# Last attention of a two-layer transformer kernel: keys and queries brought in by halves, and a new order of the work around it

## The reference

```python
x = x + attn0(_ln(x))          # 8 heads, softmax over queries
x = x + ffn_fp4(_ln(x))        # 704 wide, blockwise FP4 rounding
x = x + attn1(_ln(x))          # 16 heads of 16; q and k normalised per head
x = x + moe(_ln(x))            # base matmul + top-2 of 8 rank-16 adapters

def attn1(x):
    qkv = x @ w_qkv + b_qkv
    q = ln(q, g_q, be_q) * HD ** (-0.5);  k = ln(k, g_k, be_k)
    out = softmax(q @ k.T) @ v
    return out @ w_proj + b_proj
def moe(x):
    gate = top2(softmax(x @ R.T));  gate = gate / (gate.sum() + 1e-6)
    return x @ W.T + b + einsum(gate * (x @ A.T), B)
```

## Time and profile before

| | us |
|---|---|
| runs before, median of 3 (lowest to highest) | 3127.02 (3123.2 to 3137.87) |
| the profiled execution | 3126.74 |
| its span in the trace | 3124.9 |
| granted TensorE clock over the span | 0.96 of full speed |
| PE busy / DVE / ACT / POOL | 2703.7 / 2142.0 / 1961.6 / 1299.8 |

### The profile page before, as it was taken

How to read it: one execution, slowest core, us unless ns; L and a number is a source line. 1 busy time by engine, 2 the same in 40 slices (tenths; PEclk the granted TensorE clock), 3 DMA queues, 4 the chain that set the end, 5 groups by cost and what they waited for, 6 DMA issues and landing times.

```text
span 3124.9 us, 62704 instructions
## 1 busy us (share of the span) xinstructions
PE 2703.7 (87%) x23854; PEld 1237.8 (40%) x23854; DVE 2142.0 (69%) x4363; ACT 1961.6 (63%) x3701; POOL 1299.8 (42%) x1645
## 2 busy tenths in 40 slices
PE   4875887998899988999889988999889998998696
PEld 2433443335433444334433344334443344333232
DVE  6878766848787577856688477866779476765333
ACT  3541355875577755876568755776558755786683
POOL 4752375216732366215542166324652156412111
PEclk9987998999999999999999999999999999999797
DMA  4213241424222332224313242333323252132311
GB/s 124 60 20 61 45 97 37 80 43 104 47 68 59 70 89 71 55 41 93 82 50 76 47 108 50 75 48 74 94 57 67 34 105 56 46 67 38 83 28 27
DMA packets 474142, 201.33 MB, mean 64 GB/s; under 512 B 287561, under 2 KB 463441, under 8 KB 473817
## 3 DMA queue, kind: packets, MB, share of 16 engines
q1 hardware_dynamic: 471544, 195.12, 28.9%
q10 hardware_dynamic: 2272, 1.85, 0.2%
HBM read 46.61 MB, written 32.51 MB: 25 GB/s over the span
## 4 chain that ended last, share of the span: by engine, by line
PE 49%; DVE 26%; issue 7%; ACT 7%; POOL 4%; DMA 4%; SPq 3%; DVEq 0%; ACTq 0%; POOLq 0%
PE pV L634 10%; PE pR L425 7%; PE pS L489 7%; DVE nmaxa L1115 7%; PE pR L426 6%; PE pR L427 6%; PE pS L605 6%; ACT ub L859 4%; PE pV L522 4%; PE pR L431 2%; SPq L1774 2%; DVE ua L1027 1%; POOL ua L1570 1%; DMA xT<-xhb 1%; ACT ua L820 1%
## 5 line engine op out<-in xcount | busy, mean ns | idle before, releaser
L859 ACT ACTIVATE ub<-pS 128x512 f32<-128x512 f32 x2048 | 1047.9, 612 | 258.2 <-PE pS L605 255.2
L1115 DVE TENSOR_REDUCE nmaxa<-pS 128x1 f32<-128x1024 f32 x512 | 621.2, 1214 | 342.9 <-PE pS L489 342.1
L820 ACT ACTIVATE ua<-pS,nmaxa 128x1024 f32<-128x1024 f32 x384 | 427.6, 1113 | 519.9 <-DVE nmaxa L1115 507.7
L1570 POOL TENSOR_SCALAR ua<-ua,rz 128x256 f32<-128x256 f32 x512 | 493.3, 964 | 502.5 <-DVE rz L1132 465.1
L489 PE MATMUL pS<-ua 128*128 128x512 f16 x2048 | 545.0, 390 | 93.5 <-ACT ua L820 77.3
L634 PE MATMUL pV<-ub,vaug 128*17 128x512 f32 x4096 | 542.9, 601 | 8.5 <-DVE ub L1266 8.5
L605 PE MATMUL pS<-ub 50*128 50x512 f16 x1920 | 351.6, 385 | 41.0 <-SPq L1977 24.1
L522 PE MATMUL pV<-ua 128*32 128x128 f32 x6144 | 253.6, 285 | 53.4 <-DVE oTa L1126 33.5
L489 PEld LDWEIGHTS pS<-ua 128*128 128x128 f16 x2048 | 164.9, 99 | 337.4 <-ACT ua L820 111.4
L820 ACT ACTIVATE EA<-pS,nmaxa 128x1024 f32<-128x1024 f32 x128 | 142.5, 1114 | 169.8 <-DVE nmaxa L1115 169.8
L605 PEld LDWEIGHTS pS<-ub 50*128 50x128 f16 x1920 | 86.7, 94 | 410.0 <-ACT ub L859 315.1
(11 more groups left out here) (289 smaller groups left out, 5169.6 us busy)
## 6 DMA issues: line engine op xcount, KB each, us to landing
ua<-ua SPq DMA_DIRECT2D x384, 128.0 KB, 2.6
ub<-scr SPq DMA_DIRECT2D x276, 64.0 KB, 2.5
scr<-ub SPq DMA_DIRECT2D x30, 512.0 KB, 3.2
x<-in_L_attn_x SPq DMA_DIRECT2D x8, 1024.0 KB, 5.6
between<-x SPq DMA_DIRECT2D x7, 1024.0 KB, 5.1
ub<-between SPq DMA_DIRECT2D x7, 1024.0 KB, 5.9
out<-ub SPq DMA_DIRECT2D x7, 1024.0 KB, 5.3
ub<-scr SPq DMA_DIRECT2D x168, 32.0 KB, 1.9
```

What stands on the lines that cost most here:

```text
L820: e.activation(EA[n % 4], pS[:, 1024 * (n % 2):1024 * (n % 2) + 1024], ACT.Exp, bias=nmaxa[:, n % 32:n % 32 + 1], accum_out=zz[:, n % 8:n ...
L859: e.activation(EB[(4 * n + hl) % 8], pS[:, 512 * hl:512 * hl + 512], ACT.Exp).then_inc(e1_in, 1)
L1115: e.tensor_reduce(nmaxa[:, n % 32:n % 32 + 1], pS[:, 1024 * (n % 2):1024 * (n % 2) + 1024], AXX, ALU.max, negate=True).then_inc(max0_in, 1)
L1570: e.tensor_scalar(vs[m % 4], vv[:, :, 32 * c:32 * c + 32], rz[:, c:c + 1], None, ALU.mult).then_inc(vs_in, 1)
```

## The change

1. `heads_end` of SP brings the first 512 keys, then head group 0's first 512 queries (new `half_queries`), then the second half's tiles; `attn1` starts on the first and waits for `keys_late` at step 4 and for `fill1_late` at steps 32 and 40.
2. On DVE, `by_norm` of pairs 0 and 1 comes ahead of the Newton iteration of pairs 2 and 3 (`heads_by_end`), and the low parts are a lane of their own.
3. POOL's bias adds wait until the last low part is made.
4. PE's wait for `mrow` is on the `If` side only.
5. `second` places the mixture by a table (`at_step`) in place of the formulas.

```diff
--- before.py
+++ after.py
@@ -204,7 +204,9 @@
 
         s1_in, e1_in, pv1_in, o1_in, rc_in = (sem(n) for n in ("s1", "e1", "pv1", "o1", "rc"))
         fill1 = [sem(f"fill1_{i}") for i in range(2)]
-        fill1_end = [sem(f"fill1_end{i}") for i in range(2)]
+
+        fill1_end, fill1_late = ([sem(f"fill1_{n}{i}") for i in range(2)] for n in ("end", "late"))
+        keys_late = sem("keys_late")
         keys_in, ones_in = sem("keys"), sem("ones")
         gsm, gmax, gT, ghi, glo, mrow = (sem(n) for n in ("gsm", "gmax", "gT", "ghi", "glo", "mrow"))
 
@@ -343,10 +345,16 @@
 
 
             if b == NB - 2:
-                return [placed(lambda p: 66.5 + min(p, .43 * p + 5.4), lane(b))]
+                return [placed(lambda p: at_step(p, (66.5, 75.5, 79.5, 83.5, 89.5, 96, 103)), lane(b))]
             if b == NB - 1:
-                return [placed(lambda p: -26.8 + min(p, .42 * p + 2.9), lane(b, 0)), placed(.5, lane(b, 1))]
+                return [placed(lambda p: at_step(p, (-26, -21, -18, -13.5, -11, -7.5, 2)), lane(b, 0)), placed(.5, lane(b, 1))]
             return [lane(b)]
+
+        def at_step(p, to):
+
+            of = (0, 10, 17.7, 19.5, 30, 39, 62)
+            n = max(i for i in range(6) if p >= of[i])
+            return to[n] + (p - of[n]) * (to[n + 1] - to[n]) / (of[n + 1] - of[n])
 
         def tiles_in(hf):
             return range(NT) if hf is None else range(4 * hf, 4 * hf + 4)
@@ -559,12 +567,15 @@
                 e.wait_ge(*group_in(b, hg))
                 q, kk_ = operands(b, hg)
                 if hg == 0:
-                    e.wait_ge(keys_in, 384 * (b + 1) - (192 if b + 1 == NB else 0))
+                    e.wait_ge(keys_in, 384 * b + (384 if b + 1 < NB else 96))
                     e.wait_ge(ones_in, 2)
                 if k == 0:
                     e.wait_ge(fin, 1)
                     e.reg_load(reg, flag[0:1, 0:1])
                 with e.If_cmp(reg, 0, "IS_NE"):
+                    if b + 1 == NB and hg < 2:
+                        e.wait_ge(keys_late, 96)
+                        e.wait_ge(fill1_late[hg], 96)
                     if hg or b + 1 == NB:
                         e.wait_ge(e1_in, 256 * b + 4 * group_step(b, hg))
                     else:
@@ -580,6 +591,7 @@
                             i.then_inc(gsm, 1)
                     e.wait_ge(gmax, 32 * k + 32)
                     transpose(pS[0:32, 0:128], nmaxb[:, :]).then_inc(gT, 1)
+                    e.wait_ge(mrow, 64 * (k + 1))
                 with e.Else():
                     e.sem_inc(gsm, 32)
                     e.sem_inc(gT, 1)
@@ -592,8 +604,11 @@
                         if n == group_step(b, hg):
                             yield n - .1
                             general(b, hg)
-                            e.wait_ge(mrow, 64 * (4 * b + hg + 1))
                         yield n
+                        if b + 1 == NB and n == 4:
+                            e.wait_ge(keys_late, 96)
+                        if b + 1 == NB and n in (32, 40):
+                            e.wait_ge(fill1_late[hg], 96)
                         for hl in range(4):
 
                             if n or b + 1 == NB:
@@ -1418,12 +1433,17 @@
                     e.wait_ge(sq_in, 4 * b + tp + 1)
                     e.tensor_reduce(nve[tp // 2][:, 64 * (tp % 2):64 * (tp % 2) + 64],
                                     sqe[tp].rearrange("p (g d) -> p g d", d=16), AXX, ALU.add).then_inc(hs_in, 1)
-                    if tp == 3:
-                        e.wait_ge(hs_in, 4 * b + 4)
-                        newton(e, nr_in[1], nve[1], nye[1], nwe[1])
+                yield sums_end(3) + .3
+                e.wait_ge(hs_in, 4 * b + 4)
+                newton(e, nr_in[1], nve[1], nye[1], nwe[1])
+
+            def heads_by_end():
                 for tp in range(4):
-                    yield (sums_end(2) + .5, sums_end(3) + .2)[tp // 2]
+                    yield sums_end(3) + .1 + .4 * (tp // 2)
                     by_norm(e, tp, 0).then_inc(hmd_in, 1)
+
+            def heads_low_end():
+                b = NB - 1
                 for tp in range(4):
                     yield turn_end(tp) + .2
                     for w_ in range(2):
@@ -1530,7 +1550,7 @@
                         *([placed(-10, prep()), placed(-10, prep_low()), prep_heads()] if i < 0 else []),
                         *([v for lane in (moe_x3, moe_gate, moe_M) for v in second(i - 1, lane)] if within(i - 1) else []),
                         *([heads(i), heads_bias(i), heads_norm(i)] if within(i) and i + 1 < NB else
-                          [heads_end(), heads_bias(i), heads_norm_end()] if i + 1 == NB else [])]
+                          [heads_end(), heads_bias(i), heads_norm_end(), heads_by_end(), heads_low_end()] if i + 1 == NB else [])]
 
             phases(lanes_x, lanes_y)
 
@@ -1687,6 +1707,9 @@
                 for t in range(NT):
                     yield 20 + .1 * t
                     xb = x[b % 2][:, t, :]
+                    if t == 0:
+
+                        e.wait_ge(lo1_in, 8 * NB)
                     e.wait_ge(xh_in["H"], 8 * b + t + 1)
                     e.tensor_tensor(xb, xb, bproj[:, :], ALU.add).then_inc(xb1_in, 1)
 
@@ -1902,15 +1925,26 @@
                     yield turn_end(2 * hf + 1) + .4
                     for i in range(2):
                         e.wait_ge(spill[i], 32 * b + 16 * (hf + 1))
+                    cols = slice(512 * hf, 512 * hf + 512)
                     for par in range(2):
                         for s_ in range(3):
                             at = 64 * par + 16 * s_
-                            e.dma_start(kop[at:at + 16, :, 512 * hf:512 * hf + 512],
-                                        scr[b % 2, 1, s_ % 2, 0:128, 512 * hf:512 * hf + 512].rearrange(
-                                            "(h p d) n -> p d h n", p=2, d=16)[par]).then_inc(keys_in, 16)
-                yield 19
+                            e.dma_start(kop[at:at + 16, :, cols], scr[b % 2, 1, s_ % 2, 0:128, cols].rearrange(
+                                "(h p d) n -> p d h n", p=2, d=16)[par]).then_inc((keys_in, keys_late)[hf], 16)
+                    if hf == 0:
+                        half_queries(b, 0, 0)
+                half_queries(b, 1, 0)
                 for hg in range(2):
-                    queries(b, hg, False)
+                    half_queries(b, hg, 1)
+
+            def half_queries(b, hg, hf):
+                o, cols = 2 * (hg % 2), slice(512 * hf, 512 * hf + 512)
+                for par in range(2):
+                    for s_ in range(3):
+                        at = 64 * par + 16 * s_
+                        e.dma_start(qop[at:at + 16, o:o + 2, cols],
+                                    scr[b % 2, 0, s_ // 2, 64 * hg:64 * hg + 64, cols].rearrange(
+                                        "(h p d) n -> p d h n", p=2, d=16)[par]).then_inc((fill1, fill1_late)[hf][hg], 16)
 
             def heads(b):
                 if b:
```

## The result

| us | before | after |
|---|---|---|
| median (lowest to highest), 6 runs each, taken together | 3126.32 (3123.08 to 3137.87) | 3103.22 (3096.75 to 3112.54) |
| the profiled execution | 3126.74 | 3096.75 |
| its span | 3124.9 | 3095.0 |
| in it: from the start to the last of DVE's sums of squares (the body) | 2880.2 | 2868.2 |
| from there to the first score matmul (the gap) | 35.9 | 25.2 |

The changed kernel takes 0.9924 of the time, 95% interval 0.9900 to 0.9949: 23.1 us less, more than the 0.5% that can be told from nothing. The two profiled executions differ by 30.0 us: 12.0 in the body, 10.7 in the gap, 6.8 in the attention, 0.5 in the tail.

A forecast was written before the change was run, and what follows sets the result against it. Bound by a serial chain in the gap, then PE and ACT together in the last attention. Terms 11.5 + 5.5 + 2.2 + 0.3 + 1.9 - 0.8 - 0.9 = 19.7 us, from 3126.74 to 3107, range 3099 to 3119.

The forecast's parts named there:

- the wait for SP: Outside the last attention, PE's five idle times of 3.8 us go; half taken as gain, 1.9 us.
- my own case: Whole kernel: the main forecast, 13.4 to 24 us gained by its own bounds, 3103 to 3113; chance 0.63.
- The start: Last attention's first score matmul comes at 2904.5 where it was 2916.05, 11.5 us earlier; bounds 9.4 to 13.
- Step 4 doesn't wait: Last attention: late keys land at 2913.1, step 4's scores come at 2915.3, which leaves 2.2 us.
- the rival with the start handed back: Last attention, step 4 or later: six reads delay the late puts' landing; gain only 12 us, 3115; chance 0.17.
- The table: Last attention's mixture: gains of 5.5 (router tile), 2.2 (ghT) and 0.3 us, less 0.8 and 0.9.
- the new wait at image 7's projection: Last attention: image 7's transposes wait for image 6's base tile 7, now at step 37.0; costs 0.8 us.
- The 2.2 for ghT: Image 6's ghT: 5.4 steps from the last router tile remove the 1.76 us wait, plus 0.45 for a slow step.
- The rival "saves nothing": Last attention: PE is full and moved work lands there; only start and SP wait gain, 3115; chance 0.12.
- SP doesn't become the bound: Against the rival that slow SP reads delay image 6's transposes: 3138, decided from 0.94 us a read; chance 0.03.
- My 3.5 for this rule: In the gap, DVE's first two by_norm would take 3.5 us by the rule, not 2.8; gain 10.8.
- my terms of 0.45: Last attention: slow step behind a removed wait goes too; 0.45 us counted behind image 6's ghT, likewise at the router tile.

The follow-up runs named there:

- after_mrow_back: The changed kernel with PE's wait for mrow put back where it was: 3127.89 us, ratio 1.0000.
- act_queries: The changed kernel with the first six reads of queries issued from ACT's queue beside SP's keys: 3106.3 us, ratio 0.9935.
- late_and_table2: The changed kernel with twelve query reads behind image 6's transposes, ghT's exponential earlier for both images, image 7's projection later: 3099.0 us, ratio 0.9913.
- late_reads: The changed kernel with only the twelve reads of the queries' second half moved behind image 6's DMA transposes on SP: 3094.09 us, one execution.
- after_again: The changed kernel, unchanged, executed once more for a second trace: 3102.93 us.
- after_no_halves: The changed kernel with keys and queries read in full as before, without late waits: 3113.31 us, ratio 0.9961.
- mrow_only: The kernel before with only PE's wait for mrow moved to the If side: 3119.81 us, ratio 0.9973.
- table_only: The kernel before with only the table that places the mixture: 3123.05 us, ratio 0.9989.
- before_again: The kernel before, unchanged, executed once more for a second trace: 3130.04 us.

## Why the prediction was right, and where it was not

I forecast 3107, in a range of 3099 to 3119, and 3103.22 was measured: 19.7 us against 23.1. The mechanism of each large term was seen in the traces. That the total came so near owes something to luck: start and attention were forecast 1.8 us too high together, the wait for SP 2.3 too low. (The upper bounds of my own case add up to 24.8 and not to 24, which would have made its lower end 3102.) Step by step:

1. **The start, 11.5 forecast, 10.7 measured** (trace; 35.9 to 25.2). Counted from the last sum of squares, `by_norm`, the iteration and the low parts brought the second put 2.4 us nearer (forecast 2.05): DVE's two multiplications took 2.15 and not 2.8, and the low parts 3.35 and not 3.5. But SP's first read came 3.96 us after the second put's issue began (2881.92 to 2885.88) where I carried over the 3.28 of before. That is the step that failed: I took a landing as a constant although the two puts now start 1.2 us apart and not 2.3 (2894.04 to 2896.30 before). And the first scores came 2.46 us after the last issue where I had 2.1. The removals divide the 10.7: halves 8.3, POOL's wait 0.9, DVE's order 0.6; with the 0.6 that the wait for SP is worth alone (gap 35.3) that is 10.4. This division holds only with the wait gone: put back, it costs 14.8 us of gap (40.0).
2. **Step 4 doesn't wait**, as forecast. The late keys' puts let SP go on 6.3 us after the second's issue (2891.9 to 2898.16), not 4.66, and the rival with the start handed back came nearer than I thought: last issue near 2900.4, landed some 2 us later, needed at 2903.95. 1.5 us were left of my 2.2. The rival gave the six reads ahead of the puts as the reason. They are not: `after_mrow_back` has the same reads there, and SP goes on after 4.7 us. What the seven traces with 6.3 us have in common, and the seven others (4.7, in `act_queries` 5.3) have not at that place, is one packet of 16 KB of instructions that goes over the DMA engines while the put is under way, 2.5 to 2.7 us after PE has started the attention. The DMA engines' busy tenths, in 40 slices, and that packet in the changed kernel, from 2894 to 2899 us:

```profile
DMA  9999898999999999200000000000000000000000
...
q8 instruction: 1, 0.02, 1.2%
```

and the busy tenths in `after_mrow_back` over the same stretch of its puts, 2902.4 to 2907.4 us, which has no such packet:

```profile
DMA  9999998989999999610000000000176118613663
```

In both nearly all of the put is over some 2.1 us into the stretch. Without the packet SP goes on 0.5 us later (2904.99), with it 2.0 later (2898.16), though the engines are all but idle meanwhile. No run takes the packet away, so that it is the cause is likely and not shown.
3. **The table.** My 6.3 for the attention stands against 5.3 (162.7, the mean of two traces of before, to 157.4). The router's wait went from 4.63 to 0.58, and the new wait at image 7's projection is 0.94, forecast 0.8. **The 2.2 for ghT failed**: it waits 1.48. I counted the steps between router and ghT in PE's order, but the chain to ghT starts with the gate's exponential, and when that runs is set by its place in ACT's order. `late_and_table2` moves that place, among other edits, and the wait is gone. Without the table PE lost 7.04 us at the router tile, so the table was worth more in the changed kernel (8.0 us in the trace) than I gave it, and less alone (0.9989). The rival "saves nothing" fell.
4. **The wait for SP, 1.9 forecast.** This term was undersized. Over fourteen traces the last sum of squares starts 4.2 us earlier where the wait is gone (a fit with the time at the low clock beside it, uncertain by 0.9; last section). So about all of the 3.8 us came back, not half. Why none of it is lost to ACT, no run shows. More important is what I counted at nothing: that without this part the halves would gain nothing. I had drawn the count-up behind the reads the earlier trace rows, but never asked what each part is worth without the others.
5. **SP doesn't become the bound.** The 18 late reads took 9.24 us, 0.51 each, far from the 0.94 at which it would have decided.

The sum by what was measured: 10.7 + 5.3 + 4.2 = 20.2, of 23.1 measured with an interval of 15.9 to 31.3. The rest lies within the interval.

**A wrong reading.** The rule of the Trainium skill that I had weighed ("SBUF — State Buffer", Who interferes with whom) is that a DVE instruction with two SBUF inputs and a GpSimd instruction that reads SBUF exclude each other. I had written that the rows agree with it in direction and not in size. They agree in size too, as the multiplications of pairs 0 and 1 in the changed kernel show one by one (durations in ns, then the start):

```profile
L320 DVE TENSOR_TENSOR ua<-ua x1: 692/692/692, 2876.5 to 2876.5; 128x512 f32<-128x512 f32 x1
L320 POOL TENSOR_TENSOR ua<-ua x1: 1561/1561/1561, 2876.5 to 2876.5; 128x512 f32<-128x512 f32 x1
L320 DVE TENSOR_TENSOR ua<-ua x1: 1543/1543/1543, 2877.1 to 2877.1; 128x512 f32<-128x512 f32 x1
L320 POOL TENSOR_TENSOR ua<-ua x1: 1503/1503/1503, 2878.0 to 2878.0; 128x512 f32<-128x512 f32 x1
```

DVE, which began 0.04 us ahead, took its lone time. Then the ends come in turn, at 2877.16 (DVE), 2878.07 (POOL), 2878.62 (DVE) and 2879.54 (POOL): a duration of 1.5 us is a wait for the other engine's instruction and then the own work. My 3.5 for this rule was the order with POOL first. With DVE first its two are done after one of POOL's, which from the lone times is an estimate of 0.68 + 1.06 + 0.68 = 2.4 us, nearer to the measured 2.15 than my 2.8. So, worked out with DVE first, the rule gives a gain of 11.9 and not of 10.8, and that 10.8 lay close to the measured 10.7 was chance.

## What to carry to other kernels

An earlier start is worth only as much as the slowest in-order queue between producer and consumer lets through: here a count-up in SP's queue that nobody needed, once left in PE's path, turned 24 us of gain into none, so list for each part what it gains without the others. When a chain is moved, move the instruction that starts it on its own engine, not the one that ends it on the engine that waits. And take landing times from transfers issued at the same distance, not from the same transfers at another. When two engines slow each other, look at their instructions one by one: minimum, median and maximum hid here that they took turns.

## What the runs showed of the hardware

**A stall costs more than its length.** In the trace's clock record TensorE stood at its low level (1.2 GHz of 2.4) for 21.1 us of the attention before, 10.5 after, 23.4 without the table and 6.4 in `late_and_table2`; PE's waits in these are 8.5, 5.0, 10.7 and 0.2 us, the lengths 163.4, 156.6, 165.4 and 151.1. All begin at the low level, left over from the gap; in `late_and_table2` that first stretch is the whole 6.4, and elsewhere the rest lies around the stalls and behind them. Windows around the router's wait without the table (wait ending at 2939.42), with the granted clock after the brackets:

```profile
2930.00:2939.00 9.00, 2.33 (x16) 0.41 (x12) 4.37 (x9) 2.92 (x6) 0.00 (x0) 0.75 0.68 154
2939.00:2945.00 6.00, 5.58 (x33) 2.05 (x34) 1.06 (x6) 2.69 (x6) 0.00 (x0) 0.52 0.41 77
2945.00:2955.00 10.00, 9.79 (x90) 3.69 (x91) 4.95 (x28) 8.28 (x18) 4.02 (x7) 1.00 0.01 2
```

Behind the stall PE does 33 instructions in 6 us at 0.52, then 90 in 10 us at 1.00. The same score matmul takes 604 ns in the changed kernel's first 3 us of attention and 386 from 2911 us on:

```profile
L620 PE MATMUL pS<-ub x8: 580/604/631, 2893.4 to 2896.1; 50*128 50x512 f16 x8
L620 PE MATMUL pS<-ub x36: 376/386/387, 2911.0 to 2928.6; 50*128 50x512 f16 x36
```

A fit over the attentions of all fourteen traces gives 0.85 us of length for each us that PE waits and 0.33 for each us at the low level, and meets every length within 0.8; with the waits alone it is 1.3 us of length per us of wait. This is the "slow step" that my terms of 0.45 stood for, and why 4.8 us fewer waits could give 6.3. The low level doesn't follow from the waits alone: the second trace of before has 9.5 us of waits and only 13.5 us at it, and is 1.4 us shorter than the first.

**The body differs between executions of one order.** Before 2850 us nothing but the wait for SP differs between the kernels, yet the last sum of squares starts anywhere from 2865.7 to 2884.5. It goes with the time at the low clock before 2850 us:

| trace | low clock, us | starts at |
|---|---|---|
| late_reads | 143.4 | 2865.7 |
| after | 153.6 | 2868.2 |
| after_again | 157.0 | 2872.1 |
| after_no_halves | 167.2 | 2878.0 |
| mrow_only | 177.5 | 2879.6 |
| table_only (with the wait for SP) | 153.6 | 2876.6 |
| before (with it) | 167.2 | 2880.2 |
| before_again (with it) | 177.5 | 2884.5 |

A straight line through all fourteen gives 0.43 us per us at the low level and 4.2 for the wait. Single traces lie up to 2.3 us off this line. So of the 30.0 us between the two profiled executions 5.8 (13.6 x 0.43) are such luck, which leaves 24.2 beside the 23.1 of the medians. Why one execution falls to the low level more than another stays open.

**Transfers close together land later.** Where two puts of 512 KB start 1.2 us apart, SP goes on 3.95 to 4.19 us after the second's start (eight traces); where they start 2.3 to 2.6 apart, 3.26 to 3.29 (five traces), and 3.72 in the second trace of before. Small reads on two queues at once take 3.6 in place of 1.8.

**DVE and POOL take turns.** Beside each other, a multiplication of two SBUF tiles on DVE and one on POOL are done one after the other (1.46 us for a pair, 0.68 and 1.06 alone), and the profile counts the wait as part of the instruction. DVE's low parts beside POOL's adds go the same way: 1.21 us each, against 0.68 for the one and 0.69 for the other alone.
